# One block's output chain one scan step later, another block's keys and one value product moved, in a gated delta-rule layer on one core

## The chip, the cores and the metric

The kernel runs on one core of one Trainium2 chip. The metric is the device time of one execution in microseconds (us); the time of a kernel is the median of several executions.

## The reference

The program computes a small network on 2,048 tokens of width 128: a recurrent attention layer, a mixture of experts, a linear attention layer, and the same mixture of experts again. Every layer works on the layer norm of the residual stream and is added to it. The change touches the first layer alone:

```
def step(state, inp):
    qt, kt, vt, bt = inp
    kk = kt[..., :, None] * kt[..., None, :]
    bb = bt[..., None, None]
    state = state * (1.0 - bb * kk) + bb * (vt[..., :, None] * kt[..., None, :])
    out_t = jnp.einsum('bhij,bhj->bhi', state, qt)
    return (state, out_t)
_, outs = jax.lax.scan(step, state0, (qT, kT, vT, bT))
out = jnp.moveaxis(outs, 0, 1).reshape(b, s, nh * d)
mu = jnp.mean(out, axis=-1, keepdims=True)
var = jnp.mean((out - mu) ** 2, axis=-1, keepdims=True)
out = (out - mu) / jnp.sqrt(var + LN_EPS) * ln_g + ln_b
out = out * jax.nn.silu(x @ Wg)
return out @ Wout
```

There are 16 heads of size 8. q and k are projections divided by their norm over a head, v is a projection, beta is a sigmoid. The product of k with itself enters elementwise, so that every entry (i, j) of a head's state follows its own scalar recurrence over the tokens. The mixture of experts that follows needs, for each token, the two best of eight experts, and places its row in a table of slots with a scatter.

## The kernel before

The 2,048 tokens are cut into four blocks c of 512. A state has 16 x 8 x 8 entries: for each i of 0 to 7 the 128 pairs (head, j) lie on the partitions and the 512 tokens of a block along the rows. So there are 32 scan steps n = 8c + i, and each is written out once on every engine in a loop over n. One step n of the recurrence is:

- TensorE `repeat_v(n)`: the values, repeated for all j, into a PSUM bank (it waits for scan n - 2, which frees the bank).
- GpSimd `decay_product(n)`: the keys of index i, fetched by a DMA from a DRAM copy, times the beta keys; ScalarE `one_minus(n)` makes 1 minus that.
- VectorE `update(n)` (L1011): values times beta keys; `scan(n)` (L1020): the recurrence over 512 tokens.
- GpSimd `read_product(n)` (L502): state times q.

A block's output chain hangs on it: TensorE `sum_heads` adds the reads up, ScalarE `copy_oT` copies, TensorE `turn_o` (L1505) turns; VectorE `stats_o` (L1033), ScalarE `ln_root` (L711, into `std`), VectorE `ln_scale` (L1082 and L1084, into `rstd` and `shift`), ScalarE `normalise_o` (L699, into `otok`), TensorE `turn_n` (L1516), ScalarE `affine_nT` (L706), VectorE `open_gates` (L1040, into `gated`), TensorE `out_a`, VectorE `add_a` (L1045) and the statistics of the next layer norm, `ln_rows`, `turn_rows` (L1531), `turned_rows`, `logits`, VectorE `choose` (L1092 to L1112), TensorE `rank`, VectorE `locate` (L1118 to L1126), and at last the GpSimd scatters (L519).

The next blocks' keys are made beside it: `project_k`, `project_q`, ScalarE squares, TensorE `sum_squares` into bank 7, ScalarE `norms`, VectorE `clamp` (L970, L972), ScalarE `widen` (into `rwide`), TensorE `expand` (L1471: the norms repeated over a head), VectorE `unit_k` (L991) and `beta_k` (L998). Behind `unit_k` the DMA queue of SyncE copies the keys to DRAM and fetches the eight decays of the block.

The order on every engine is that of its loop, written out by hand. `due(n, after, first)` gives the block b with n = 8b + after, so that `due(n, 10)` puts the block's statistics in steps 10, 18, 26, 34. Within TensorE's loop body the order is `out_a`, `repeat_v`, `sum_squares`, the logits, `sum_heads`, `expand`, `turn_o`, `rank`, `turn_n`, `project_k`, `project_q`, the gate's product of steps 7 to 10, `turn_rows`. `repeat_v(n + 1)` stands in step n, but for `repeat_v(10)`, which stands in step 8. Waits that tie the chains together: `sum_squares(3)` waits for `ln_scale` of block 0's second norm (bank 7), `turn_n(1)` for `locate` of block 0 (bank 5), and on GpSimd the second four scatters of block 1 for `locate` of block 2. `PUTS` gives each scatter of a block its step: 24 to 29 for block 0; those of the other blocks stand behind the scan.

Of the kernel before, what the change touches and what calls it, by code (L numbers as in the profile page):

```python
# [27 lines left out]
HD = D // H  # L28
# [6 lines left out]
NSTEP = NB * HD  # L35
# [37 lines left out]
def program(nc, x, Wq, Wk, Wv, Wbeta, Wg, Wout, ln_g, ln_b, W_qkv, proj, W_out, b_out, w_g, c_fc, c_proj, out):  # L73
# [8 lines left out]
    with ctx:  # L82
# [83 lines left out]
        with ExitStack() as mb:  # L166
# [21 lines left out]
            b = mb.enter_context(ExitStack())  # L188
# [92 lines left out]
        last_state = lambda n: ps[:, (0, 2)[n - NSTEP + N_LAST], :]  # L281

        def due(n, after, first=0):
            b, late = divmod(n - after, HD)
            return b if late == 0 and first <= b < NB else None

# [666 lines left out]
        def _(dve):  # L953
# [13 lines left out]
            def clamp(c):  # L967
                dve.wait_ge(norm_ready, part_done(c, 1))
                dve.wait_ge(wide_ready, 2 * c)
                dve.tensor_scalar(flat(rnorm[:]), norms_in, 1e-12, None, ALU.max).then_inc(rn_clamped, 1)  # L970
                dve.wait_ge(rn_clamped, part_done(c, 1))
                dve.reciprocal(rnorm[:], rnorm[:]).then_inc(rn_ready, 1)  # L972
# [10 lines left out]
            def first_decay(i):  # L983
                dve.wait_ge(krep_ready, i + 1)
                dve.tensor_tensor(decay[:, i, :], ps[:, 6, :], bkT[:, 0, :], ALU.mult).then_inc(first_made, 1)
# [22 lines left out]
            def update(n):  # L1008
                c = n // HD
                dve.wait_ge(vrep_ready, n + 1)  # L1010
                dve.tensor_tensor(ps[:, 3 + n % 2, :], ps[:, 3 + n % 2, :], bkT[:, c % 2, :],  # L1011
                                  ALU.mult).then_inc(update_ready, 1)

            def scan(n):
                i = n % HD
                dve.wait_ge(decay_ready, n + 1)
                dve.wait_ge(update_ready, n + 1)
                if n >= HD:
                    dve.wait_ge(read_ready, n - HD + 1)
                dve.tensor_tensor_scan(out=state[:, i, :] if n < NSTEP - N_LAST else last_state(n), data0=decay[:, i, :], data1=ps[:, 3 + n % 2, :],  # L1020
                                       initial=state[:, i, BK - 1:BK], op0=ALU.mult,
                                       op1=ALU.add).then_inc(scan_done, 1)

            def read_last(n):
                dve.wait_ge(scan_done, n + 1)
                dve.wait_ge(out_ready, 2 * (NB - 2) + 2)
                dve.tensor_tensor(read[:, n % HD, :], last_state(n), qT[:, (NB - 1) % 2, :],
                                  ALU.mult).then_inc(last_read, 1)
# [48 lines left out]
            def ln_scale(n, c, moments=None):  # L1077
                tt = slice(TB * c, TB * c + TB)
                mean = mv[:, tt, 0] if moments is None else moments[:, :, 0]
                done = blocks_past(n) + (c + 1 if n < 4 else c - NB + 3)  # L1080
                dve.wait_ge(ln_std[n], done)
                dve.reciprocal(rstd[:, tt], std[:, tt]).then_inc(ln_rstd[n], 1)  # L1082
                dve.wait_ge(ln_rstd[n], done)
                dve.scalar_tensor_tensor(out=shift[:, tt], in0=mean, scalar=-1.0, in1=rstd[:, tt],  # L1084
                                         op0=ALU.mult, op1=ALU.mult).then_inc(ln_shift[n], 1)
# [63 lines left out]
            for n in range(NSTEP + 10 + HD):  # L1149
                if n < NSTEP:  # L1150
                    update(n)
                    if n == 17:
                        clamp(3)
                    scan(n)
                if n == 11:
                    ln_scale(1, 0, moments_o)
                if n == NSTEP - 1:
                    for late in range(NSTEP - N_LAST, NSTEP):
                        read_last(late)
                if n == 0:  # L1160
                    first_decay(1)
                    clamp_half(0, 0)
                if n == 1:
                    clamp_half(1, 1)
                    unit_q(0)
                if n == 2:
                    unit_k(1)
                if n == 3:
                    clamp_half(1, 0)
                if n == 4:  # L1170
                    beta_k(1)
                if n == 5:
                    unit_q(1)
                b = due(n, 17)
                if b is not None:
                    choose(0, b, logits_in(5), marks_in(5))
                b = due(n, 10)
                if b is not None:
                    stats_o(b)
                b = due(n, -6, 2)  # L1180
                if b is not None:
                    unit_k(b)
                    beta_k(b)
                b = due(n, 10)
                if b is not None and 0 < b < NB - 1:
                    ln_scale(1, b, moments_o)
                b = due(n, 18)
                if b is not None:
                    locate(0, b, ps[:, 5 if b < NB - 1 else 4, P:2 * P].rearrange("p (r t e) -> p r t e", r=4, e=NE),
                           ps[:, 5, 3 * P:3 * P + 4 * TB].rearrange("p (r t) -> p r t", r=4))  # L1190
                b = due(n, 10)
                if b == NB - 1:
                    ln_scale(1, b, moments_o)
                    normalise_late()
                b = due(n, 12)
                if b is not None:
                    open_gates(b)
                b = due(n, -3, 2)
                if b is not None:
                    unit_q(b)  # L1200
                b = due(n, 13)
                if b is not None:
                    add_a(b)
                    ln_stats(2, b, moments_a)
                b = due(n, 14)
                if b is not None:
                    ln_scale(2, b, moments_a)
                    if b == NB - 1:
                        rows_late_part(2)
                if n == 8:  # L1210
                    clamp(2)
# [201 lines left out]
        def _(pe):  # L1413
# [226 lines left out]
            for n in range(NSTEP + 10 + HD):  # L1640
                b = due(n, 13)
                if b is not None:
                    out_a(b)
                    if b == NB - 1:
                        keep_warm(30, 1)
                if 1 < n + 1 < NSTEP and n != 9:
                    repeat_v(n + 1)
                if n == 8:
                    repeat_v(n + 2)
                b = due(n, -9, 2)  # L1650
                if b is not None:
# [20 lines left out]
                b = due(n, 16)  # L1672
# [4 lines left out]
                b = due(n, 8)  # L1677
                if b is not None:
                    sum_heads(b, 1)
                b = due(n, -7, 2)  # L1680
                if b is not None:
                    expand(b)
                b = due(n, 9)
                if b is not None:
                    turn_o(b)
                b = due(n, 17)
# [4 lines left out]
                b = due(n, 11)  # L1691
# [6 lines left out]
                b = due(n, HD + -3)  # L1698
# [6 lines left out]
                b = due(n, -10, 2)  # L1705
# [18 lines left out]
                b = due(n, 15)  # L1724
# [102 lines left out]
            for gp in range(2):  # L1827
                for a_ in range(2):
                    n = 2 * gp + a_
# [103 lines left out]
```

## Time and profile before

| | |
|---|---|
| median of 3 runs | 478.07 us (477.09 to 481.09) |
| the profiled execution | 480.44 us, of which the span from its first to its last instruction is 478.6 us |
| TensorE busy | 416.2 us (87%) |
| VectorE busy | 311.5 us (65%) |
| GpSimd busy | 264.6 us (55%) |
| ScalarE busy | 235.0 us (49%) |
| mean granted clock of TensorE | 0.951 of full speed |

The rows of a trace give the start from the beginning of the span, the duration, the engine and the line of the instruction (a helper's line where a helper issues it), the tile that it writes and those that it reads, and the shapes. In square brackets stands the idle time of that engine just before, and what ended it. Engines are PE (TensorE), PEld (its weight loads), DVE (VectorE), ACT (ScalarE), POOL (GpSimd). Matmuls are pipelined: the next one starts some tenths before the recorded end of the last, and an f32 product appears as two instructions (x2).

### The profile page before, as it was taken

The page shows a single profiled execution, that of the slowest core. Times are in us where ns is not written, and L with a number is a line of the kernel's source. Part 1 is how long each engine was busy: PE and PEld are TensorE (multiplying, and loading weights), DVE is VectorE, ACT ScalarE, POOL GpSimd, SP SyncE. Part 2 cuts the span into 40 slices and gives each one's busy share as a digit, 9 for nine tenths or more (in the row PEclk, how much of TensorE's full clock was granted, in tenths as well). Part 3 has the DMA queues.
Part 4 walks back from the last instruction along what each step waited for, and adds up shares of the span by engine and source line. Part 5 has one row for each costly group of instructions (what it writes and reads, how often), then busy time and mean ns, then how long its engine had stood idle before and what let it go on. Part 6 is the DMA issues. An engine that isn't in the chain of part 4 may idle for free.

```text
span 478.6 us, 8009 instructions
## 1 busy us (share of the span) xinstructions
PE 416.2 (87%) x2850; PEld 302.3 (63%) x2850; DVE 311.5 (65%) x740; ACT 235.0 (49%) x367; POOL 264.6 (55%) x329
## 2 busy tenths in 40 slices
PE   7888796877898999999988999889878979999970
PEld 5544353333698899999964333345356969999960
DVE  5898799999753232525595999899985602421274
ACT  4777755413330355344058998878763105334320
POOL 4999675897677956465409200020656723456470
PEclk9999897775999999999999999999998999999995
DMA  5447571992161222225524444496011121232376
GB/s 144 151 163 262 165 253 53 316 322 77 41 227 50 73 85 62 68 74 207 160 83 104 100 99 100 121 285 211 24 34 46 56 80 43 59 88 61 94 241 202
DMA packets 50327, 60.88 MB, mean 127 GB/s; under 512 B 7152, under 2 KB 29296, under 8 KB 50288
## 3 DMA queue, kind: packets, MB, share of 16 engines
q1 hardware_dynamic: 42672, 47.50, 33.3%
q0 software_dynamic: 4608, 8.47, 5.5%
q10 hardware_dynamic: 3008, 4.40, 2.8%
q8 instruction: 23, 0.38, 0.3%
q14 instruction: 16, 0.13, 0.1%
HBM read 29.78 MB, written 25.31 MB: 115 GB/s over the span
## 4 chain that ended last, share of the span: by engine, by line
PE 44%; POOL 10%; issue 6%; DVE 6%; DMA 5%; ACT 4%; POOLq 0%; DVEq 0%; ACTq 0%
PE ps L1415 39%; POOL slots_x L519 8%; DVE feat L1337 3%; PE ps L1571 2%; DMA last_got<-chosen_y 1%; PE ps L1419 1%; DMA chosen_y<-ye,y_to 1%; DMA xe<-slots_x 1%; ACT expo L878 1%; POOL chosen_y L569 1%; DMA slots_x<-rows_x,put_at 1%; ACT xnT L621 1%; DVE stats L1071 1%; ACT rows_x L723 1%; POOLq L82 0%
## 5 line engine op out<-in xcount | busy, mean ns | idle before, releaser
L569 POOL DMA_INDIRECT chosen_y<-ye,y_to x80 | 79.3, 991 | 67.5 <-DVE ye L1287 48.0
L1337 DVE SCALAR_TENSOR_TENSOR feat<-expo,ps 128x1024 f32<-128x1024 f32 x64 | 76.4, 1217 | 5.6 <-ACT expo L878 5.2
L762 ACT ACTIVATE hT<-ps 128x640 f32<-128x640 f32 x64 | 45.1, 705 | 69.6 <-PE ps L1415 69.6
L519 POOL DMA_INDIRECT slots_x<-rows_x,put_at x64 | 62.9, 983 | 27.1 <-issue 16.9
L878 ACT ACTIVATE expo<-ps,minus_one 128x1024 f32<-128x1024 f32 x64 | 70.4, 1115 | 11.6 <-PE ps L1415 7.9
L1415 PE MATMUL ps<-cproj_sb,hT 128*128 128x128 f32 x640 | 74.6, 276 | 0.2
L1415 PEld LDWEIGHTS ps<-cproj_sb,hT 128*128 128x128 f32 x640 | 73.0, 192 | 0.6 <-ACT hT L762 0.6
L1419 PE MATMUL ps<-ident 128*128 128x128 f32 x546 | 66.1, 280 | 7.2 <-DMA slots_x<-rows_x,put_at 3.4
L1237 DVE TENSOR_TENSOR xe_low<-ps,xeT 128x640 fp32r<-128x640 f32 x16 | 13.2, 825 | 86.0 <-ACT xeT L621 86.0
L1419 PEld LDWEIGHTS ps<-ident 128*128 128x128 f32 x546 | 62.1, 145 | 9.7 <-DMA slots_x<-rows_x,put_at 4.3
L502 POOL TENSOR_TENSOR read<-state,qT 128x512 f32<-128x512 f32 x30 | 37.9, 1268 | 16.4 <-DVE state L1020 16.3
L1415 PE MATMUL ps<-xnT,wv_rep 128*128 128x512 f32 x64 | 40.1, 718 | 4.5 <-DVE state L1020 4.5
L1020 DVE TENSOR_TENSOR_SCAN state<-decay,state,ps 128x512 f32<-128x512 f32 x30 | 38.3, 1277 | 3.2 <-DVE ps L1011 0.5
L493 POOL TENSOR_TENSOR decay<-decay,bkT 128x512 f32<-128x512 f32 x30 | 37.8, 1267 | 0.4 <-DMA decay<-k_rows 0.4
L584 POOL TENSOR_SCALAR var_eps<-mv 128x4 f32<-128x4 f32 x2 | 0.5, 232 | 63.8 <-DVE mv L1074 63.8
L1415 PE MATMUL ps<-xeT,cfc_high 128*128 128x320 f32 x128 | 32.5, 335 | 1.9 <-ACT xeT L621 1.9
L1287 DVE TENSOR_TENSOR ye<-ps,slot_w 128x256 f32<-128x256 f32 (+2 forms) x38 | 16.6, 439 | 26.3 <-PE ps L1415 25.5
L621 ACT ACTIVATE xeT<-ps 128x640 fp32r<-128x640 f32 x16 | 11.2, 699 | 38.5 <-PE ps L1571 38.5
L1415 PE MATMUL ps<-xe_low,cfc_high 128*128 128x320 f32 x128 | 29.4, 310 | 0.0
L1415 PE MATMUL ps<-xeT,cfc_low 128*128 128x320 f32 x128 | 29.2, 309 | 0.0
L1415 PE MATMUL ps<-stk,pstk 97*128 97x512 f32 x64 | 22.6, 441 | 4.4 <-DVE feat L1337 4.3
L1415 PE MATMUL ps<-pstk,stk 97*128 97x512 f32 x64 | 23.4, 449 | 1.2 <-DVE part L1317 0.9
(238 smaller groups left out, 702.3 us busy)
## 6 DMA issues: line engine op xcount, KB each, us to landing
chosen_y<-empty_rows SPq DMA_DIRECT2D x32, 256.0 KB
decay<-k_rows SPq DMA_DIRECT2D x30, 256.0 KB, 4.8
stk<-part SPq DMA_DIRECT2D x96, 64.0 KB, 2.0
slots_x<-empty_rows SPq DMA_DIRECT2D x16, 325.0 KB, 5.9
xe<-slots_x SPq DMA_DIRECT2D x16, 325.0 KB, 2.9
cfc_sb<-in_L_ffn_c_fc SPq DMA_DIRECT2D x2, 2048.0 KB, 9.6
got<-chosen_y SPq DMA_DIRECT2D x8, 256.0 KB, 4.9
got<-chosen_y ACTq DMA_DIRECT2D x8, 256.0 KB, 5.9
```

The lines of the kernel that those rows point to most:

```text
L493: pool.tensor_tensor(decay[:, i, :], decay[:, i, :], bkT[:, c % 2, :], ALU.mult).then_inc(product_ready, 1)
L502: pool.tensor_tensor(read[:, i, :], state[:, i, :], qT[:, c % 2, :], ALU.mult).then_inc(read_ready, 1)
L519: pool.indirect_dma_start(out=slots_x[k], out_offset=bass.IndirectOffsetOnAxis(ap=put_at[:, c, kk, t:t + 1], axis=0), in_=rows_x[:, kk * N ...
L569: pool.indirect_dma_start(out=chosen_y[k], out_offset=bass.IndirectOffsetOnAxis(ap=y_to[:, b, i:i + 1], axis=0), in_=ye[:, b, i * D:(i + 1 ...
L621: copy = lambda o, i: act.activation(o, i, ACT.Copy)
L762: act.activation(hT[:, b, f, :].rearrange("p (a n) -> p a n", a=2), ps[:, 2 + 2 * (f % 2):4 + 2 * (f % 2), 0:HALF], ACT.Gelu).then_inc(h_r ...
L878: act.activation(expo[:, g % 3, :], flat(ps[:, pair, :]), ACT.Exp, bias=minus_one[:]).then_inc(f_exp, 1)
L1020: dve.tensor_tensor_scan(out=state[:, i, :] if n < NSTEP - N_LAST else last_state(n), data0=decay[:, i, :], data1=ps[:, 3 + n % 2, :], ini ...
L1287: dve.tensor_tensor(ye[:, b, i0 * D:i1 * D].rearrange("p (i d) -> p i d", d=D), ps[:, bank_of(s, n), 0:(i1 - i0) * D].rearrange("p (i d) - ...
L1337: dve.scalar_tensor_tensor(out=feat[:, g % 4, :], in0=expo[:, g % 3, :], scalar=1.0, in1=flat(ps[:, pair, :]), op0=ALU.min, op1=ALU.max).t ...
L1415: return pe.matmul(o, lhsT, rhs, start=start, stop=stop, **kw)
L1419: pe.transpose(ps[:, bank, 0:P], ident[:], ident[:])
```

## The change

Three things move, and no instruction is added or dropped.

- `due` gives, for `after` of 10 and more, block 0 one step later: everything of block 0 from `stats_o` to the scatters moves by one step on all engines (`ln_scale` of its first norm from step 11 to 12, `turn_n` from 11 to 12, `open_gates` from 12 to 13, `out_a` and `add_a` from 13 to 14, the next norm's `ln_scale` from 14 to 15, `choose` from 17 to 18, `locate` from 18 to 19, the scatters from 24 to 29 into 25 to 30). The other blocks keep their steps.
- `unit_k` and `beta_k` of block 2 move from step 10 to step 11.
- `repeat_v(11)` moves on TensorE from step 10 to step 9, ahead of `expand(2)`, `turn_o(0)` and the gate's product there.

```diff
@@ -281,6 +281,8 @@
         last_state = lambda n: ps[:, (0, 2)[n - NSTEP + N_LAST], :]
 
         def due(n, after, first=0):
+            if after >= HD + 2 and n - after < HD:
+                return 0 if n - after == 1 and first == 0 else None
             b, late = divmod(n - after, HD)
             return b if late == 0 and first <= b < NB else None
 
@@ -1152,7 +1154,7 @@
                     if n == 17:
                         clamp(3)
                     scan(n)
-                if n == 11:
+                if n == 12:
                     ln_scale(1, 0, moments_o)
                 if n == NSTEP - 1:
                     for late in range(NSTEP - N_LAST, NSTEP):
@@ -1177,7 +1179,7 @@
                 b = due(n, 10)
                 if b is not None:
                     stats_o(b)
-                b = due(n, -6, 2)
+                b = 2 if n == 11 else due(n, -6, 3)
                 if b is not None:
                     unit_k(b)
                     beta_k(b)
@@ -1643,9 +1645,9 @@
                     out_a(b)
                     if b == NB - 1:
                         keep_warm(30, 1)
-                if 1 < n + 1 < NSTEP and n != 9:
+                if 1 < n + 1 < NSTEP and n not in (9, 10):
                     repeat_v(n + 1)
-                if n == 8:
+                if n in (8, 9):
                     repeat_v(n + 2)
                 b = due(n, -9, 2)
                 if b is not None:
```

## Rows read from the trace of the kernel before

**Rows 1.** The chain that ended last (start, us, what): the end of routing.

```profile
152.95 2.41 DMA slots_x<-rows_x,put_at
```

**Rows 2.** Timeline (start, us, engine, line) of GpSimd, steps 12, 26 and behind the scan.

```profile
53.12 1.26 POOL L502 TENSOR_TENSOR read<-state,qT 128x512 f32<-128x512 f32 x1 [3.00 <-DVE state L1020]
...
105.56 1.28 POOL L502 TENSOR_TENSOR read<-state,qT 128x512 f32<-128x512 f32 x1
...
128.62 0.96 POOL L519 DMA_INDIRECT slots_x<-rows_x,put_at  x1 [2.50 <-DVE put_at L1126]
```

**Rows 3.** Timeline of VectorE, steps 9 to 12.

```profile
43.09 1.28 DVE L1020 TENSOR_TENSOR_SCAN state<-decay,state,ps 128x512 f32<-128x512 f32 x1
...
45.05 1.28 DVE L1020 TENSOR_TENSOR_SCAN state<-decay,state,ps 128x512 f32<-128x512 f32 x1
48.48 0.89 DVE L1033 BATCH_NORM_STATS2 stats<-ps 128x6 f32<-128x128 f32 x4 [2.15 <-PE ps L1505]
...
51.77 1.28 DVE L1020 TENSOR_TENSOR_SCAN state<-decay,state,ps 128x512 f32<-128x512 f32 x1
...
53.80 0.61 DVE L1084 SCALAR_TENSOR_TENSOR shift<-mean_var,rstd 128x4 f32<-128x4 f32 x1
...
57.68 0.69 DVE L1040 TENSOR_TENSOR gated<-ps,gate 128x512 f32<-128x512 f32 x1 [1.30 <-ACT ps L706]
```

**Rows 4.** What VectorE waited for, 46 to 131 us: total, times, longest.

```profile
DVE stats L1033 <- PE ps L1505: 2.1, 1, 2.1
DVE gated L1040 <- ACT ps L706: 1.3, 1, 1.3
DVE rstd L1082 <- ACT std L711: 0.9, 2, 0.5
```

**Rows 5.** Timeline of VectorE, steps 17 and 26.

```profile
69.31 0.70 DVE L1011 TENSOR_TENSOR ps<-ps,bkT 128x512 f32<-128x512 f32 x1 [0.44 <-PE ps L1415]
...
104.88 3.20 DVE L1084 SCALAR_TENSOR_TENSOR shift<-mean_var,rstd 128x4 f32<-128x4 f32 x1
```

**Rows 6.** Timeline of TensorE, steps 8 to 16.

```profile
44.53 1.02 PE L1415 MATMUL ps<-xnT,wgate 128*128 128x512 f32 x2
...
51.14 1.02 PE L1415 MATMUL ps<-xnT,wv_rep 128*128 128x512 f32 x2
55.16 1.29 PE L1516 MATMUL ps<-ident,otok 128*128 128x128 f32 x4 [3.00 <-ACT otok L699]
56.29 1.89 PE L1415 MATMUL ps<-xnT,wv_rep 128*128 128x512 f32 x2
57.96 1.90 PE L1415 MATMUL ps<-xnT,wall 128*128 128x512 f32 x2
...
65.75 1.85 PE L1415 MATMUL ps<-head_of,squares 128*128 128x16 f32 x16
...
68.25 1.02 PE L1415 MATMUL ps<-xnT,wv_rep 128*128 128x512 f32 x2
```

**Rows 7.** Timeline of ScalarE, steps 9 to 12.

```profile
47.60 0.63 ACT L681 ACTIVATE decay<-decay 128x512 f32<-128x512 f32 x1
...
54.44 1.63 ACT L699 ACTIVATE otok<-ps,shift,rstd 128x128 f32<-128x128 f32 x4 [0.89 <-DVE shift L1084]
...
56.89 0.76 ACT L706 ACTIVATE ps<-ps,lnb,lng 128x512 f32<-128x512 f32 x1
```

**Rows 8.** The instructions of L1084: duration min/median/max in ns, first and last start, forms.

```profile
L1084 DVE SCALAR_TENSOR_TENSOR shift<-mean_var,rstd x4: 161/384/3198, 53.8 to 128.5; 128x4 f32<-128x4 f32 x4
```

**Rows 9.** Busy time by stretch; third number from the right: the granted clock.

```profile
55.00:59.50 4.50, 4.30 (x8) 1.91 (x9) 3.02 (x5) 3.19 (x8) 3.10 (x3) 0.65 0.92 280
```

**Rows 10.** Timeline of TensorE, steps 19 and 20.

```profile
80.93 1.14 PE L1516 MATMUL ps<-ident,otok 128*128 128x128 f32 x4 [1.68 <-DVE put_at L1126]
82.92 2.08 PE L1415 MATMUL ps<-xnT,wv_rep 128*128 128x512 f32 x2 [0.84 <-DVE state L1020]
```

**Rows 11.** DMA issues of the whole span: KB each, median us to landing.

```profile
decay<-k_rows SPq DMA_DIRECT2D x30, 256.0 KB, 4.8
```

## The prediction

> **What bounds the kernel now.** I read the chain that ended last first. It runs without a break from the scan's last steps through block 3's output chain into the scatters, the last of which is issued at 152.95 [rows 1]; everything behind that (experts, linear attention, experts) hangs on those slots and simply moves with them. GpSimd's scatters are back to back from 128.62 on, after a wait of 2.50 for `locate` of block 2 on VectorE [rows 2]. So a microsecond that VectorE gains or loses in steps 10 to 31 goes through to the end, as long as GpSimd reaches that wait early.
>
> Then VectorE's waits: in the scan it is the engine with hardly a gap. A step with nothing beside update and scan takes 1.96 (scan starts at 43.09 and 45.05) [rows 3]. The only long waits are 2.1 for `turn_o(0)` in step 10, 1.3 for `affine_nT(0)` in step 12 and 0.5 for `ln_root(1, 0)` in step 11 [rows 4], in all 4.0. They are what moving block 0's chain touches. A fourth loss is no wait in that list: in step 26 a VectorE instruction on four elements per partition takes 3.20 [rows 5].
>
> **Part 1: step 10 emptied, `repeat_v(11)` earlier.** Scan 10 ends at 46.33 (45.05 + 1.28), and VectorE then idles 2.15 [rows 3]. In the new order `update(11)` comes next. Its values stand right behind the gate's product (44.53 to 45.55), so they are there at about 46.4, and the update ends at 47.1 [rows 6]. But scan 11 also needs `one_minus(11)`, which ScalarE does at 47.60 to 48.23, behind `widen(2)` and `copy_oT(0)`; nothing in the change moves these [rows 7]. So scan 11 starts at 48.27, with some 1.1 of new waiting. Then the statistics and keys that left step 10: from 48.48 to scan 11's update they took 2.50 (scan 11 starts at 51.77, its update 0.79 earlier at 50.98) [rows 3]; new, 49.47 + 2.50 = 51.97. `update(12)` finds `repeat_v(12)` done at 52.16, since it still stands behind the last gate product [rows 6]: 0.2 more. New waits 1.3 to 1.4 against 2.15: **gain 0.8**. Bounds: 0 (if `one_minus(11)` slips by as much again) and 2.15.
>
> **Part 2: `ln_scale(1, 0)` in step 12.** The wait of 0.54 for `std` goes: with scan 12 at 53.0 to 54.3, ScalarE has had time to load its table. Yet I count no gain. In the trace the small L1084 takes 0.61 from 53.80 and ends at 54.41, with GpSimd's read product (53.12 to 54.38) [rows 2, 3]; it reads two tiles of SBUF and was held until that read was over. The read is started by the scan's end, in the new order too, and ends 1.33 behind it. So scan end to `shift` stays 1.36. Bounds: 0 and a gain of 1.0 (0.54, and the 0.45 by which 0.61 is above the shortest, 0.16 [rows 8]), if GpSimd is late.
>
> **Part 3: `open_gates(0)` in step 13.** From `shift` (54.41) over `otok` (54.44), `turn_n` (55.16), affine (56.89) to the gate (57.68) it is 3.27 [rows 3, 6, 7]; VectorE has one bare step of 1.96 to fill it, before and after, since `ln_scale` moved by the same step as the gate. The wait of 1.30 stays: **0**. Bounds: 0 and 1.3.
>
> **Part 4: what stands behind `turn_n(0)` on TensorE.** Before, only `repeat_v(13)` stood between `turn_n(0)` and the next use by VectorE; it was over (58.18) when the gate was (58.37). New, `turn_n(0)` is in step 12 behind `repeat_v(13)`, and `project_k(3)` and `repeat_v(14)` come after it. In the new order `shift` is out at 55.63, so `turn_n` runs from 56.4 to 57.6, and the two products take 1.9 each at the lower clock, with a pitch of 1.7 (56.29 to 57.96) [rows 6], to 61.1. VectorE is done with the gate at 59.6 and with `unit_q(2)`, of about that size, at 60.1. **Loss 1.0.** The stretch 55.0 to 59.5 had a granted clock of 0.65 of full speed, mostly the 1.2 GHz level, after 3.00 without a matmul [rows 6, 9]; the new gap is 3.4, so I take the lower level. At 2.4 GHz the products take 1.02 each and the loss is 0. Bounds 0 and 1.0.
>
> **Part 5: `sum_squares(3)`, `repeat_v(17)`, `choose(0)`.** `sum_squares(3)` waits for block 0's second `ln_scale`, now in step 15 after scan 15. It takes 1.85, and `repeat_v(17)` 1.02 behind it [rows 6]. I get `update(17)` 0.85 late where it was 0.44 [rows 5]: loss 0.4. `choose(0)` in step 18 finds logits that hang on `turned_rows`, on ScalarE now behind `widen(3)`, which waits for `clamp(3)` of step 17: loss 0.25. **Loss 0.65**, bounds 0 and 1.3 (each twice).
>
> **Part 6: `turn_n(1)` behind `locate(0)`.** It was released by `locate(0)` in step 18 at 80.93, and `repeat_v(21)` had still to wait 0.84 for scan 19 [rows 10]. With `locate(0)` in step 19, both products (1.14 and, at the lower clock, 2.08, pitch 0.9 and 2.0) lie between `locate` and `update(21)`; VectorE has 1.96 for a bare step and 0.6 for the gate. **Loss 0.5**, bounds 0 and 0.5.
>
> **Part 7: scatters one step later.** The 3.20 of L1084 in step 26 starts at 104.88, while GpSimd runs scatter, read (105.56), decay product without a gap; it ends at 108.08, with the decay product [rows 2, 5]. Block 0's first three scatters are in front of it now, two after the change. GpSimd is released by scan 22 in both orders, so its offset to VectorE in step 26 is fixed: it is one scatter (1.26) ahead, and at 104.88 is 0.6 into the read, to be over at 105.6. As in part 2, L1084 then ends with that read, after 0.75: **gain 2.45**. If it is also passed over by the decay product behind, it ends at 106.8: gain 1.2. Bounds: a loss of 0.7 (a wait longer than any in the trace by that) and 3.04 (no wait). The Trainium skill (SBUF — State Buffer, Who interferes with whom) says that an instruction with two SBUF inputs contends with a GpSimd instruction that reads SBUF, and that the loser is blocked for the whole of that one instruction. The 0.61 agrees with it, the 3.20, which spans two product instructions and half a scatter, doesn't; by the rule this part gains 2.45, by the longer row 1.2 or less.
>
> The scatters are still all issued. One more now lies between scan 27 and GpSimd's wait, 1.3 and its issue gap 0.3, against a wait of 2.50 [rows 2]: 0.9 is left, so this costs nothing. If that cover were gone, each scatter too late would cost 1.3. The block's `k_rows` copy and decay DMAs on SyncE's queue start 1.0 later with `unit_k(2)`, but with the copy's 2 and a decay's 4.8 [rows 11] the first lands by 59, and scan 16 starts near 68: 0.
>
> **Sum.** 0.8 - 1.0 - 0.65 - 0.5 + 2.45 = 1.1 us less. The profiled span of 478.6 (480.44 with what lies around it) becomes 477.5; on the median of 478.07 it is **477.0**. That is no change that a measurement of this kernel can tell, which begins at about 1%, 4.8 us.
>
> **Rivals.**
> - *The held instruction is passed over again, slower:* in step 26 L1084 isn't served at the end of the read product, as in the row of 3.20, and waits 3 us once more. Then part 7 is 0 and the sum is a loss of 1.35: 479.4. It decides from a duration of 2.1 upwards in step 26 (1.1 of gain used up). For it: the same instruction at the same place did so. Against it: GpSimd is elsewhere in its sequence, and in step 11 it was served at once. Chance 0.27.
> - *TensorE keeps 2.4 GHz in steps 12 to 20:* parts 4 and 6 cost nothing: 475.5. For it: the lower clock lasted only until 59.5, and a clock that rises 1 us earlier suffices for part 4. Against it: the gap ahead of `turn_n(0)` grows. Chance 0.15.
> - *The waits go, as the change says:* parts 1 to 3 give 2.15 + 1.0 + 1.3, the losses of parts 4 to 6 hide, part 7 gives 2.45: 6.9 less, 471.2. Against it: `one_minus(11)` and the chain `shift` to gate don't move. Chance 0.10.
> - *Nothing moves but the place of the waits:* part 7 small (1.2), part 1 eaten by 4 to 6: 478.2. Chance 0.10.
>
> **How the numbers follow.** The forecast has 0.38, and its own range from the half-known parts 4 and 7 is 475.5 to 478.5. The range of 8 in 10 reaches to the slower rival and its spread and to the warm clock with part 1 whole: 473.8 to 480.0; the third rival is left out below it. Faster by over 1% is the third rival and a little of the second: 0.11. Slower by over 1% needs the slower rival and GpSimd late for `locate` too: 0.05. Within 1%: 0.84.
>
> **What would show it.** In the changed kernel's VectorE timeline: scan 11 some 1 us behind `update(11)`, released by ScalarE's decay; L1084 of block 0 ending with a read product; 1.3 ahead of L1040; an update in step 14 waiting for TensorE with the granted clock below 1; L1084 of step 26 at 0.7. I am wrong if block 0's L1084 takes 0.16, if the gate's wait shrinks, if the update of step 14 doesn't wait, or if L1084 in step 26 is again above 2.

## The result: 489.4 us, 1.9% slower, and the profile after

The changed kernel takes 489.37 us (median of 4 runs, 486.14 to 490.18) where the kernel before took 478.42 beside it (4 runs): a ratio of 1.0186 on record, with an interval of 1.0144 to 1.0227 (the quotient of these two medians alone would be 1.023). The prediction was 477.0, with a range that ended at 480.0. Lines of the changed file are those of before plus 2 (L1020 is L1022, L1084 is L1086, L1415 is L1417).

The start of a scan on VectorE's timeline cuts the span into stretches. These are the profiled executions of both kernels:

| stretch, us | before | after | difference |
|---|---|---|---|
| up to scan 10 | 45.05 | 46.83 | +1.78 |
| scan 10 to 16 | 22.54 | 23.72 | +1.18 |
| scan 16 to 22 | 22.83 | 27.09 | +4.26 |
| scan 22 to 31 | 30.14 | 30.31 | +0.17 |
| scan 31 to the end | 358.04 | 360.45 | +2.41 |
| span | 478.6 | 488.4 | +9.8 |

VectorE's timeline of the changed kernel (start, us, engine, line; in brackets the idle time before and its releaser), in the order of the prediction's parts:

```profile
50.05 1.28 DVE L1022 TENSOR_TENSOR_SCAN state<-decay,state,ps 128x512 f32<-128x512 f32 x1 [1.12 <-ACT decay L683]
...
54.06 0.70 DVE L1013 TENSOR_TENSOR ps<-ps,bkT 128x512 f32<-128x512 f32 x1 [0.38 <-PE ps L1417]
...
56.23 1.25 DVE L1086 SCALAR_TENSOR_TENSOR shift<-mean_var,rstd 128x4 f32<-128x4 f32 x1
...
60.77 0.69 DVE L1042 TENSOR_TENSOR gated<-ps,gate 128x512 f32<-128x512 f32 x1 [1.30 <-ACT ps L708]
...
63.14 0.70 DVE L1013 TENSOR_TENSOR ps<-ps,bkT 128x512 f32<-128x512 f32 x1 [1.08 <-PE ps L1417]
...
65.76 0.69 DVE L1047 TENSOR_TENSOR xres<-ps,xres 128x512 f32<-128x512 f32 x1 [0.55 <-PE ps L1417]
...
74.59 0.70 DVE L1013 TENSOR_TENSOR ps<-ps,bkT 128x512 f32<-128x512 f32 x1 [2.76 <-PE ps L1417]
...
78.60 0.70 DVE L1013 TENSOR_TENSOR ps<-ps,bkT 128x512 f32<-128x512 f32 x1 [1.04 <-PE ps L1417]
...
87.36 1.28 DVE L1022 TENSOR_TENSOR_SCAN state<-decay,state,ps 128x512 f32<-128x512 f32 x1 [0.45 <-issue]
...
92.53 0.70 DVE L1013 TENSOR_TENSOR ps<-ps,bkT 128x512 f32<-128x512 f32 x1 [0.23 <-PE ps L1417]
...
106.96 3.52 DVE L1109 TENSOR_TENSOR_SCAN upto<-later_tile,chosen 128x64 bf16<-128x64 f32 x1
...
114.23 0.95 DVE L1086 SCALAR_TENSOR_TENSOR shift<-mean_var,rstd 128x4 f32<-128x4 f32 x1
```

The last scatter of routing follows scan 31 by the same 32.4 in both orders (120.56 to 152.95 before, 127.95 to 160.35 after), so what is lost up to scan 31 goes through to it, and the 2.41 at the end come in the experts and the linear attention behind it.

The two rows with the large numbers were not in the sum as they came out: `update(17)` at 74.59 waits 2.76, where it waited 0.44 before [rows 5], and L1109, a prefix sum of 64 elements in `choose(1)`, takes 3.52 in step 25. TensorE's timeline, with its gaps at `turn_n(0)` (58.24) and `sum_squares(3)` (70.00), stands behind the first:

```profile
58.24 1.45 PE L1518 MATMUL ps<-ident,otok 128*128 128x128 f32 x4 [3.43 <-ACT otok L701]
59.48 1.92 PE L1417 MATMUL ps<-xnT,wall 128*128 128x512 f32 x2
61.19 1.91 PE L1417 MATMUL ps<-xnT,wv_rep 128*128 128x512 f32 x2
...
67.28 1.02 PE L1417 MATMUL ps<-xnT,wv_rep 128*128 128x512 f32 x2
70.00 2.66 PE L1417 MATMUL ps<-head_of,squares 128*128 128x16 f32 x16 [1.70 <-DVE shift L1086]
72.50 2.05 PE L1417 MATMUL ps<-xnT,wv_rep 128*128 128x512 f32 x2
74.48 1.94 PE L1417 MATMUL ps<-read,headsum 128*32 128x512 f32 x8
```

`sum_squares(3)` took 1.85 and the values behind it 1.02 before [rows 6]; now they take 2.66 and 2.05. Busy time by stretch (the third number from the right is the granted clock), after:

```profile
66.00:70.00 4.00, 2.30 (x6) 0.78 (x5) 3.84 (x14) 2.32 (x4) 2.12 (x3) 1.00 0.87 288
70.00:74.00 4.00, 4.00 (x18) 2.98 (x18) 1.74 (x2) 1.60 (x5) 4.00 (x4) 0.62 0.53 153
74.00:78.00 4.00, 4.00 (x15) 1.45 (x14) 2.94 (x4) 2.53 (x6) 0.96 (x2) 0.52 0.00 0
```

and before, over the same work:

```profile
63.40:75.40 12.00, 10.28 (x66) 6.12 (x64) 11.14 (x26) 8.99 (x18) 9.92 (x8) 1.00 0.52 146
```

So behind the gap of 1.70 the clock falls from 2.4 GHz to nearly the 1.2 GHz level; in the kernel before no such gap stands there, and it stays up. The second large row has GpSimd beside it; its timeline in the changed kernel:

```profile
58.82 1.27 POOL L495 TENSOR_TENSOR decay<-decay,bkT 128x512 f32<-128x512 f32 x1 [1.35 <-DMA decay<-k_rows]
...
106.58 1.21 POOL L521 DMA_INDIRECT slots_x<-rows_x,put_at  x1 [0.19 <-issue]
107.82 1.28 POOL L504 TENSOR_TENSOR read<-state,qT 128x512 f32<-128x512 f32 x1
109.04 1.27 POOL L495 TENSOR_TENSOR decay<-decay,bkT 128x512 f32<-128x512 f32 x1
...
112.68 1.25 POOL L504 TENSOR_TENSOR read<-state,qT 128x512 f32<-128x512 f32 x1 [1.19 <-DVE state L1022]
113.90 1.25 POOL L495 TENSOR_TENSOR decay<-decay,bkT 128x512 f32<-128x512 f32 x1
...
136.11 0.96 POOL L521 DMA_INDIRECT slots_x<-rows_x,put_at  x1 [1.63 <-DVE put_at L1128]
```

L1109 is asked for at 106.96, 0.38 into the first scatter, and ends at 110.48, with the decay product (109.04 + 1.27 = 110.31) and not before it. That is what L1084 did in step 26 of the kernel before [rows 5]: it ended at 108.08, its decay product at 108.05. L1107 met a product there. VectorE of the kernel before, step 25:

```profile
100.05 0.77 DVE L1107 TENSOR_TENSOR_SCAN upto<-later_tile,chosen 128x64 bf16<-128x64 f32 x1
```

and its GpSimd, the product that L1107 met, the scatter that L1084 met and the product with which L1084 ended:

```profile
99.38 1.28 POOL L493 TENSOR_TENSOR decay<-decay,bkT 128x512 f32<-128x512 f32 x1
...
104.53 1.01 POOL L519 DMA_INDIRECT slots_x<-rows_x,put_at  x1 [0.17 <-issue]
...
106.78 1.27 POOL L493 TENSOR_TENSOR decay<-decay,bkT 128x512 f32<-128x512 f32 x1
```

In the changed kernel the same small instruction of step 26 (114.23) is asked for during a product (113.90) and ends with it. GpSimd had waited 1.19 for scan 26 there, which step 25 had made late.

### The profile page after: what moved, and what is told of

Read it like the earlier page. It is cut to its first block, busy times and chain, and to the rows that moved or that the text cites. A ratio compares the mean times of both kernels' runs of the same rounds, so it can differ in the third digit from the quotient of the medians.

```text
span 488.4 us, 8009 instructions
## 1 busy us (share of the span) xinstructions
PE 420.8 (86%) x2850; PEld 306.4 (63%) x2850; DVE 313.7 (64%) x740; ACT 234.9 (48%) x367; POOL 264.5 (54%) x329
## 4 chain that ended last, share of the span: by engine, by line
PE 45%; DVE 10%; ACT 6%; DMA 5%; POOL 5%; issue 3%; ACTq 0%; POOLq 0%; DVEq 0%
PE ps L1417 40%; DVE feat L1339 4%; POOL slots_x L521 4%; PE ps L1573 2%; PE ps L1421 2%; ACT expo L880 2%; DMA last_got<-chosen_y 1%; ACT rows_x L725 1%; DMA chosen_y<-ye,y_to 1%; DMA xe<-slots_x 1%; POOL chosen_y L571 1%; DMA slots_x<-rows_x,put_at 1%; ACT xnT L623 1%; DVE stats L1073 1%; DVE xres L1366 1%
## 5 line engine op out<-in xcount | busy, mean ns | idle before, releaser
L1417 PE MATMUL ps<-cproj_sb,hT 128*128 128x128 f32 x640 | 74.6, 275 | 0.3
L1421 PE MATMUL ps<-ident 128*128 128x128 f32 x546 | 68.7, 287 | 6.5 <-POOL head_of L442 2.3
L1417 PEld LDWEIGHTS ps<-cproj_sb,hT 128*128 128x128 f32 x640 | 72.9, 192 | 0.6 <-ACT hT L764 0.6
L1421 PEld LDWEIGHTS ps<-ident 128*128 128x128 f32 x546 | 64.6, 149 | 8.8 <-DMA slots_x<-rows_x,put_at 2.9
L1417 PE MATMUL ps<-xnT,wv_rep 128*128 128x512 f32 x64 | 40.3, 726 | 2.4 <-DVE state L1022 2.4
L1022 DVE TENSOR_TENSOR_SCAN state<-decay,state,ps 128x512 f32<-128x512 f32 x30 | 38.3, 1276 | 4.5 <-ACT decay L683 1.1
L1417 PE MATMUL ps<-xeT,cfc_high 128*128 128x320 f32 x128 | 32.3, 334 | 1.9 <-ACT xeT L623 1.9
L1417 PE MATMUL ps<-xe_low,cfc_high 128*128 128x320 f32 x128 | 29.4, 311 | 0.0
L1417 PE MATMUL ps<-xeT,cfc_low 128*128 128x320 f32 x128 | 29.1, 309 | 0.0
L1013 DVE TENSOR_TENSOR ps<-ps,bkT 128x512 f32<-128x512 f32 x32 | 22.0, 687 | 7.5 <-PE ps L1417 7.2
L1417 PE MATMUL ps<-stk,pstk 97*128 97x512 f32 x64 | 22.6, 440 | 4.3 <-DVE feat L1339 4.3
```

What stands on the lines that cost most here:

```text
L1417: return pe.matmul(o, lhsT, rhs, start=start, stop=stop, **kw)
L1421: pe.transpose(ps[:, bank, 0:P], ident[:], ident[:])
```

## Experiments

Stretches on VectorE in every profiled execution, with the medians and ratios to the kernel before on the same chip. The kernel before had a median of 480.03 beside warm_squares, free_squares, after_no_lock and before_no_lock, of 480.67 beside before_again, after_again, old_scatters and after_best, and of 480.16 beside the other four. Where medians of different groups are compared below, up to 0.64 of the difference lies in that.

| kernel | scan 10 starts | 10 to 16 | 16 to 22 | 22 to 31 | sum 10 to 31 | rest | median | ratio |
|---|---|---|---|---|---|---|---|---|
| before | 45.05 | 22.54 | 22.83 | 30.14 | 75.51 | 358.04 | 478.42 | 1 |
| before_again | 46.06 | 23.37 | 22.89 | 27.07 | 73.33 | 358.51 | 481.85 | 1.0026 [0.9981, 1.0071] |
| after | 46.83 | 23.72 | 27.09 | 30.31 | 81.12 | 360.45 | 489.37 | 1.0186 [1.0144, 1.0227] |
| after_again | 48.67 | 23.92 | 27.09 | 30.41 | 81.42 | 359.11 | 488.46 | 1.0161 [1.0117, 1.0204] |
| warm_squares | 48.52 | 23.89 | 24.33 | 30.08 | 78.30 | 357.68 | 485.59 | 1.0130 [1.0093, 1.0167] |
| free_squares | 47.28 | 23.82 | 24.38 | 30.02 | 78.22 | 357.80 | 485.37 | 1.0112 [1.0011, 1.0213] |
| after_warm | 47.01 | 21.90 | 25.47 | 29.88 | 77.25 | 359.54 | 486.36 | 1.0126 [1.0059, 1.0193] |
| old_scatters | 48.73 | 23.92 | 27.10 | 27.09 | 78.11 | 358.96 | 483.04 | 1.0065 [1.0009, 1.0120] |
| after_no_lock | 47.27 | 21.67 | 24.49 | 29.13 | 75.29 | 359.54 | 483.87 | 1.0071 [1.0030, 1.0112] |
| before_no_lock | 48.49 | 22.19 | 22.90 | 27.10 | 72.19 | 359.02 | 480.72 | 1.0000 [0.9960, 1.0041] |
| after_best | 45.04 | 21.91 | 22.98 | 26.86 | 71.75 | 358.91 | 479.92 | 0.9978 [0.9937, 1.0019] |
| before_best | 45.43 | 22.18 | 22.66 | 27.25 | 72.09 | 358.38 | 478.74 | 0.9974 [0.9931, 1.0017] |
| before_warm | 45.13 | 22.54 | 23.78 | 30.12 | 76.44 | 358.33 | 479.34 | 0.9977 [0.9941, 1.0012] |
| after_best_warm | 46.10 | 20.86 | 23.42 | 28.22 | 72.50 | 359.30 | 479.00 | 0.9965 [0.9931, 0.9998] |

### Which of it repeats: both kernels once more

No edit.

> The changed kernel, once more, for its size with many runs and a second trace. Theory (the loss lies in steps 11 to 20 and is there in every execution): from scan 10 to scan 31 81.1 again, 5.6 more than before, with update(17) waiting over 2 and the small scan of step 25 at 3.5. Rival (the loss is a bad draw of the clock in one profiled execution): 78 or less, and a ratio under 1.01.

> The kernel before, once more, for a second trace of it. In the profiles so far all kernels share steps 0 to 8, yet scan 10 starts at 45.05 in the trace of before and at 46.8 to 48.5 in five others, where TensorE ran at the lower clock for a stretch around 24 to 34 us. Theory draw (when the clock drops in the first 40 us differs from execution to execution of the same program): scan 10 at 46.8 to 48.5 here too, the stretch from scan 10 to scan 31 again 75.5. Rival (the changed kernel is slower there for a reason of its own): scan 10 at 45.05 again.

Scan 16 to 22 is 27.09 in both executions of the changed kernel and 22.8 to 22.9 in both of the kernel before: this loss belongs to the change. Scan 10 to 16 is less clear: it differs by 0.83 between the two executions of the kernel before. Scan 22 to 31 shows what one profile had hidden. Before, it takes 30.14 in one execution and 27.07 in the other. The row of 3.20 that the prediction took for a fixed cost of the kernel before is missing in the second. VectorE's timeline of before_again, steps 25 and 26:

```profile
101.63 1.09 DVE L1107 TENSOR_TENSOR_SCAN upto<-later_tile,chosen 128x64 bf16<-128x64 f32 x1
...
106.47 0.16 DVE L1084 SCALAR_TENSOR_TENSOR shift<-mean_var,rstd 128x4 f32<-128x4 f32 x1
```

and of GpSimd there:

```profile
106.43 1.01 POOL L519 DMA_INDIRECT slots_x<-rows_x,put_at  x1 [0.17 <-issue]
```

L1084 is asked for 0.04 behind the scatter's start and gets through in 0.16; in the first execution it was asked for at 104.88, 0.35 behind a scatter that started at 104.53, and was held for 3.20. So a third of a microsecond decides over three. Of the three profiles of the old order with these instructions untouched, two hold L1084 for 3.20 (before and before_warm, below) and one doesn't. The changed kernel shows a held L1109 (3.52) and 30.3 to 30.4 in both of its executions.

### The gap ahead of `sum_squares(3)`: fill it, or take it away

warm_squares puts 14 transposes of the identity into the gap; free_squares gives the statistics of the second norm another PSUM bank, so that `sum_squares(3)` no longer waits for `ln_scale` of step 15:

```diff
+                if c == 3:
+                    keep_warm(14, 5)
                 pe.wait_ge(sq_ready, part_done(c, 1))
```

```diff
-        moments_a = ps[:, 7, 0:2 * TB].rearrange("p (t m) -> p t m", m=2)
+        moments_a = ps[:, 2, 0:2 * TB].rearrange("p (t m) -> p t m", m=2)
...
-                    pe.wait_ge(ln_shift[2], c - 2)
+                    pe.wait_ge(xres_a, c - 2)
```

> The changed kernel with 14 dummy transposes on TensorE in front of sum_squares(3) of step 15, in the gap of 1.70 us that its profile shows there. Theory clock (the gap drops the granted clock, and the products behind it run at the lower level): the clock stays at 1.0 from 66 to 78 us, sum_squares takes 1.85 instead of 2.66, repeat_v(17) 1.02 instead of 2.05, update(17) waits about 1 instead of 2.76, update(18) 0 instead of 1.04; some 2.5 to 3 us faster than the changed kernel. Theory order (what counts is that sum_squares(3) must wait for ln_scale of block 0 and stands in front of repeat_v(17)): update(17) waits 2 or more, and the time is that of the changed kernel.

> The changed kernel with the second norm's moments in bank 2 instead of bank 7, so that sum_squares(3) waits for add_a(0) only, not for ln_scale. Theory order: sum_squares(3) starts 1.1 us earlier (it then waits for its squares), update(17) waits 1.6 instead of 2.76. Theory clock: the gap falls to 0.6 us and with it the drop of the clock, so that update(17) waits under 1 and update(18) not at all: 3 us faster than the changed kernel. Neither touches step 25.

TensorE's timeline of warm_squares:

```profile
71.86 1.93 PE L1417 MATMUL ps<-head_of,squares 128*128 128x16 f32 x16 [0.17 <-DVE shift L1086]
73.64 1.10 PE L1417 MATMUL ps<-xnT,wv_rep 128*128 128x512 f32 x2
```

and VectorE's:

```profile
74.78 0.70 DVE L1013 TENSOR_TENSOR ps<-ps,bkT 128x512 f32<-128x512 f32 x1 [1.09 <-PE ps L1417]
```

With the gap filled the clock stays at 1.00 of full speed over 68.6 to 77.6, `update(17)` waits 1.09 instead of 2.76, `update(18)` not at all, and scan 16 to 22 falls from 27.09 to 24.33. As `sum_squares` itself starts no earlier in its step, these 2.8 us are the clock's. The median falls by 2.9. What is left of `update(17)`'s wait, 1.09, is the late start. In free_squares the gap shrinks to 0.61:

```profile
69.46 1.96 PE L1417 MATMUL ps<-head_of,squares 128*128 128x16 f32 x16 [0.61 <-ACT squares L653]
71.27 1.69 PE L1417 MATMUL ps<-xnT,wv_rep 128*128 128x512 f32 x2
```

The clock falls here too (0.74 over 69.4 to 76.0), but the products start sooner and the result is the same, 24.38. So the clock fell behind a gap of 0.61 here. It need not: in after_best, below, the same gap of 0.61 stands there, and the values behind it take 1.10. Nor need it behind the 1.70: after_no_lock, below, has that gap and keeps the clock.

### The gap ahead of `turn_n(0)`

after_warm has the transposes of warm_squares, and 28 more ahead of `turn_n(0)`:

```diff
                         pe.wait_ge(gate_ready, NB)
+                        keep_warm(28, 5)
                     turn_n(b)
```

> The changed kernel with dummy transposes in both long gaps of TensorE, 28 ahead of turn_n(0) in step 12 and 14 ahead of sum_squares(3) in step 15; its order is that of the change. Theory clock (what the changed order loses in steps 11 to 20 is the lower clock behind these two gaps): update(14) waits under 0.3 instead of 1.08 and add_a(0) not at all; from scan 10 to scan 22 46.5 instead of 50.8, near the 45.4 to 46.3 of before. Theory order: 48 as with the second gap alone.

```profile
58.34 1.39 PE L1520 MATMUL ps<-ident,otok 128*128 128x128 f32 x4 [0.30 <-ACT otok L701]
59.56 1.02 PE L1417 MATMUL ps<-xnT,wall 128*128 128x512 f32 x2
```

The two products behind `turn_n(0)` take 1.02 each instead of 1.92 and 1.91. `update(14)` and `add_a` no longer wait, and scan 10 to 16 falls by 2.0 from 23.89 to 21.90. Scan 16 to 22 gives 1.1 of that back: 0.72 of the gap ahead of `sum_squares(3)` is left behind the 14 transposes, the granted clock is 0.58 from 71.2 to 75.3, and `update(18)`, besides `update(17)`, waits 1.10. So scan 10 to 22 takes 47.37, 0.85 less than in warm_squares, where 1.7 was expected. The median, 486.36, does not show it.

### Block 0's scatters back in their old steps

```diff
-                b = due(n, 24)
+                b = 0 if n == 24 else None
...
-                    b = due(n, 24 + late)
+                    b = 0 if n == 24 + late else None
```

> The changed kernel with block 0's scatters in their old steps 24 to 29 on GpSimd, all else as changed. Theory (what the small VectorE instructions of steps 25 and 26 are held by is set by where the scatters stand): the small scan of step 25 takes 0.8 as in before and ln_scale's product of step 26 3.2; from scan 22 to scan 31 30.1 as in before, and the time is that of the changed kernel within 1 us, since one wait replaces the other. Rival (the 3.52 comes from elsewhere in the changed order): it stays above 2 with the old scatters.

VectorE's timeline, step 25:

```profile
109.06 1.09 DVE L1109 TENSOR_TENSOR_SCAN upto<-later_tile,chosen 128x64 bf16<-128x64 f32 x1
```

and GpSimd's beside it:

```profile
108.72 1.27 POOL L495 TENSOR_TENSOR decay<-decay,bkT 128x512 f32<-128x512 f32 x1
```

L1109 now meets the decay product and not the scatter, and ends with it. Scan 22 to 31 is 27.09, 3.3 less than in after_again, with scan 10 to 22 as it was (51.02 and 51.01). The median falls by 5.4 (four runs, 480.77 to 487.58), of which the profile accounts for 3.3. So the hold of L1109 comes with the moved scatters. The expectation that 3.20 in step 26 would take its place missed: L1086 is asked for 0.04 behind a scatter's start (113.90 and 113.86) and takes 0.16, as in before_again. So against an execution of the old order that passes there the second loss is 3.3, and against one that is held, as in the two first profiles, it is 0.2.

### Which instructions are held: one SBUF input instead of two

In both orders, L1084 (L1086) and L1107 (L1109) get a copy of one operand in PSUM:

```diff
+                later = flat(later_tile[:])
+                if k == 0 and c == 1:
+                    later = ps[:, 2, 2 * P:2 * P + 64]
+                    dve.tensor_copy(later, flat(later_tile[:]))
...
-                                       data0=flat(later_tile[:]),
+                                       data0=later,
```

That is the half for the prefix sum; in `ln_scale` of blocks 0 to 2 a second reciprocal writes the operand to PSUM.

> The changed kernel with one of the two SBUF inputs of ln_scale (blocks 0 to 2) and of choose's second scan (block 1) put into PSUM, by an extra reciprocal or copy of 0.2 us. Theory port (these small VectorE instructions are held while GpSimd's products read SBUF): the scan of step 25, 3.52 in the changed kernel, takes 0.3, ln_scale's product 0.16 in every block; 3 to 4 us faster than the changed kernel. Rival (the 3.52 has another cause, such as the scatter running then): it stays above 1 us.

> The kernel before with the same replacement. Theory port: the 3.20 of step 26 becomes 0.16 and the 0.77 of step 25 0.3; 2.5 to 3 us faster than before, 475.5. Rival (other cause): the time of before.

VectorE's timeline of after_no_lock:

```profile
103.19 0.29 DVE L1117 TENSOR_TENSOR_SCAN upto<-ps,chosen 128x64 bf16<-128x64 f32 x1
103.40 2.84 DVE L1122 TENSOR_TENSOR rows_x<-eight 128x4 f32<-128x4 f32 x2
```

and GpSimd's:

```profile
102.39 1.21 POOL L521 DMA_INDIRECT slots_x<-rows_x,put_at  x1 [0.17 <-issue]
103.63 1.29 POOL L504 TENSOR_TENSOR read<-state,qT 128x512 f32<-128x512 f32 x1
104.85 1.28 POOL L495 TENSOR_TENSOR decay<-decay,bkT 128x512 f32<-128x512 f32 x1
```

The prefix sum, with one input from PSUM, passes in the middle of the scatter in 0.29. The next instruction, whose two inputs both lie in SBUF, is held instead, to the end of the decay product. So at the same point of GpSimd's sequence it is the two SBUF inputs that count, not the operation. In step 26 and in block 0's `ln_scale` the instruction takes 0.16 in both orders.

The place counts too. Behind the scan, where scatters follow each other with no product behind them, the same prefix sum with both inputs in SBUF passes inside a scatter. GpSimd and VectorE of the kernel before:

```profile
125.15 0.97 POOL L519 DMA_INDIRECT slots_x<-rows_x,put_at  x1 [0.30 <-issue]
...
125.81 0.29 DVE L1107 TENSOR_TENSOR_SCAN upto<-later_tile,chosen 128x64 bf16<-128x64 f32 x1
```

It is asked for 0.66 into that scatter; in eleven profiles it was 0.21 to 0.82 into one, and took 0.29 each time. So the scatter alone holds nothing; the long holds came only where products stood behind it.

Not all that the changed kernel gains here is the hold. Scan 10 to 16 gains 2.2: L1086 is done 1.1 earlier, the gap ahead of `turn_n(0)` shrinks from 3.44 to 2.42, and the lower clock behind it ends sooner, so that `update(14)` waits 0.60 instead of 1.08 and `add_a` not at all instead of 0.75. And scan 16 to 22 falls from 27.09 to 24.49 with the gap of 1.70 still there:

```profile
68.39 1.93 PE L1425 MATMUL ps<-head_of,squares 128*128 128x16 f32 x16 [1.70 <-DVE shift L1090]
70.17 1.10 PE L1425 MATMUL ps<-xnT,wv_rep 128*128 128x512 f32 x2
```

The granted clock is 1.00 from 68.3 to 73.7, and `update(17)` waits 1.09, as in warm_squares. That bears out that the clock, and not the order, makes the difference between 27.1 and 24.4; and it shows that the gap alone doesn't decide whether the clock falls. What else does is open. In the old order the expected 475.5 missed: the median, 480.72, is level with that of the kernel before (1.0000).

### Both losses undone at once

after_best adds a PSUM copy for the held subtraction and the edit of free_squares, and moves `project_k(3)` behind the values of step 14; before_best has the PSUM copies in the old order, with the early transposes of the next section:

```diff
+                twin = eight
+                if k == 0 and c == 1:
+                    twin = ps[:, 2, 3 * P:3 * P + TB * NE].rearrange("p (t e) -> p t e", e=NE)
+                    dve.tensor_copy(twin, eight[:])
...
-                                      eight[:, :, 1 - kk], ALU.subtract)
+                                      twin[:, :, 1 - kk], ALU.subtract)
...
-                if n == 12:
+                if n == 13:
                     project_k(3)
```

> The changed kernel with sum_squares(3) freed of the wait for ln_scale, project_k(3) of step 12 put behind repeat_v(14), and all three small VectorE instructions with two SBUF inputs (ln_scale's product, choose's second scan and its subtractions in step 25) given one input in PSUM. Theory (clock and port are the whole of the loss): update(14) and update(17) wait under 0.8, steps 25 and 26 hold nothing above 0.5, from scan 10 to scan 31 under 72.5, that is 3 less than before and 8.6 less than the changed kernel; 477 to 478. Rival (more is lost in the moved chain): 74 and more, 480 and more.

> The kernel before with these transposes and with one input of the small VectorE instructions of steps 11 to 26 in PSUM. Theory port and draw: scan 10 near 45.1, from scan 10 to scan 31 72.2 as in the profile with PSUM inputs alone; 475.5. Rival (the wait of 3.20 was rare in before): 478 as with the transposes alone.

In VectorE's timeline of after_best nothing is held in step 25:

```profile
99.80 0.29 DVE L1121 TENSOR_TENSOR_SCAN upto<-ps,chosen 128x64 bf16<-128x64 f32 x1
100.00 0.20 DVE L1126 TENSOR_TENSOR rows_x<-eight,ps 128x4 f32<-128x4 f32 x2
```

Scan 10 to 31 takes 71.75, 9.7 less than in after_again, and the median, 479.92, is back at that of the kernel before. So what these edits remove is the loss. The move of `project_k(3)` has no run of its own. The moved chain brings no gain that these profiles show: with its costs gone it stands at 71.75 and 72.50 (after_best_warm, below), and the old order, with the same copies, at 72.09 (before_best).

### The start of the scan: filling TensorE's early gaps

Steps 0 to 8 are the same code in all kernels, yet scan 10 starts between 45.0 and 48.7. The granted clock in 20 to 28 us, in after_again:

```profile
20.00:28.00 8.00, 7.08 (x31) 4.70 (x31) 6.18 (x10) 4.49 (x11) 6.67 (x6) 0.79 0.59 189
```

and in after_best:

```profile
20.00:28.00 8.00, 6.50 (x32) 3.86 (x32) 7.17 (x11) 5.35 (x12) 7.58 (x7) 1.00 0.54 163
```

The execution with 0.79 starts scan 10 at 48.67, the one with 1.00 at 45.04; before_no_lock, in the old order, has 0.79 too, and 48.49. All 14 profiles fall into three groups: a clock of 0.79 in 20 to 28 and in 28 to 36 goes with 48.5 to 48.7 (four), 0.79 in 28 to 36 alone with 46.8 to 47.3 (four, the first profile of the changed kernel among them), and 1.00 in both with 45.0 to 46.1 (six). The next two kernels fill the gaps there with transposes:

```diff
                 if n == 0:
+                    keep_warm(8, 5)
                     expand(0, (0,))
...
                 if n == 3:
+                    pe.wait_ge(xnT_ready[0], NB)
+                    keep_warm(11, 6)
```

> The kernel before with 8 and 11 dummy transposes in TensorE's gaps of 0.92 and 1.27 us in steps 0 and 3. Theory draw (the kernels' spread of several us is the clock, which drops behind these gaps in some executions): scan 10 at 45.0 to 45.4 where eight profiles gave 45.0 to 48.7, granted clock 1.0 in all of 8 to 44 us, and the runs' spread halves, median 478 to 479. Rival (the draw has another cause): scan 10 anywhere up to 48.7, the spread of before.

> The changed kernel with sum_squares(3) freed, project_k(3) behind repeat_v(14), the PSUM inputs, and the transposes of steps 0 and 3. If the clock and the port were all that the change lost: from scan 10 to scan 31 71.8 as without the transposes, scan 10 near 45.1, 475.5 and level with the kernel before under the same remedies. Rival (the moved chain has a gain of its own that they uncover): 1 us or more below that kernel.

Scan 10 starts at 45.13 and 46.10 (45.43 in before_best, which has them too). That fits, in three profiles, but the medians hardly move, and the 475.5 expected of before_best and after_best_warm missed by 3. after_best_warm is below the kernel before by 0.35%, with an interval that ends 0.02% short of no change: I don't call that a faster version.

## Why the prediction was wrong

| part | forecast | measured in the profile of after against before |
|---|---|---|
| 1 step 10 emptied | -0.8 | waits 1.12 + 0.38 for 2.15: -0.65 |
| 2 `ln_scale` of block 0 | 0 | wait of 0.54 gone, L1086 1.25 for 0.61: +0.1 |
| 3 gate of block 0 | 0 | 1.30, as before: 0 |
| 4 behind `turn_n(0)` | +1.0 | `update(14)` 1.08, and `add_a` 0.55 |
| 5 `sum_squares(3)` | +0.65 | `update(17)` 2.76 for 0.44, `update(18)` 1.04: +3.4 |
| 6 behind `locate(0)` | +0.5 | `update(21)` +0.23, and 0.45 ahead of scan 19 |
| 7 step 26 | -2.45 | L1086 0.95 for 3.20: -2.25; L1109 3.52 for 0.77 in step 25: +2.75 |

**Parts 1 to 4 held in the main.** Scan 11 is released by ScalarE's decay with a wait of 1.12 (forecast 1.04); block 0's L1086 (56.23) ends with the read product; the gate waits 1.30; `update(14)` waits 1.08 with its two products at the lower clock. What was missing is `add_a`'s 0.55 (0.75 in after_again): the lower clock went one product further, into `sum_heads`. The cover named in part 7 held too: the copies of the keys made GpSimd wait 1.35 at 58.82, three steps ahead of need, and its wait for `put_at` still has 1.63 of the 2.50 [rows 2].

**Part 5 failed, in its size.** It saw that `sum_squares(3)` would wait for `ln_scale`, and priced the lateness of two products at 1.85 and 1.02. It didn't ask what TensorE does until then. The engine is through at 68.30 and idles 1.70, and part 4 had already read from [rows 6, 9] what comes behind a gap: the lower level. With 2.66 and 2.05 instead, and `sum_heads` at 1.94, the wait is 2.76 and reaches the next update as well. warm_squares shows 2.8 us of it to be the clock, and with the clock up the part comes out near its forecast of 0.65: `update(17)` waits 1.09 for 0.44, and `choose(0)` 0.24, which the later updates hid in the changed kernel. That the clock would fall could not be read from the gap with certainty (after_no_lock); it fell in after, after_again, old_scatters and free_squares.

**Part 7 failed, in its place.** The number for the instruction itself came out (0.7; it is 0.95), but by luck: the offset to GpSimd that the part took as fixed was gone, GpSimd waited 1.19 for scan 26, and L1086 ended with the decay product and not with the read. Two things more were wrong around it. The 3.20 that was to be saved is there in one execution of the kernel before and absent in another, so that against before_again nothing is saved. And the part followed one instruction only. Each instruction with two SBUF inputs that VectorE runs in steps 24 to 30 had to be set against the new order of scatters and products. L1107 stood in the trace with 0.77, where 0.29 is its time alone, ending with a product: the sign that it contends. With the sequence shifted it meets a scatter and is held for 3.52. The Trainium skill (SBUF — State Buffer, Who interferes with whom) lets the loser wait for one instruction of GpSimd. Requests during a product agree (0.95, 1.09, 1.25); those inside a scatter with products behind it don't (2.84, 3.20, 3.52): by its rule each of them would have been over within 1.3, an estimate from the products' 1.25 to 1.30.

**The rivals.** The nearest was the held instruction that is passed over again. Its mechanism came, but in step 25, where no rival looked, and together with part 5. The chance of 0.05 for slower was too small: it asked for two mishaps at once in named places, and two did come in others. The first rival's boundary of 2.1 stands too high: 0.75 and the 1.1 of gain make 1.85. It decided nothing.

**What adds up and what doesn't.** Scan 10 to 31 costs 5.6 more in the two first profiles, and 8.1 more between after_again and before_again. The medians differ by 7.8 (again) and 11. The rest lies ahead of scan 10 and behind scan 31, where the code is the same and executions of either order differ by up to 3.7 and 2.8. Without the early transposes scan 10 starts later than 46.1 in seven of eight profiles of the changed order and in one of three of the old one; whether the changed order makes late starts likelier isn't settled by so few. Nor is the 0.45 ahead of scan 19, or why GpSimd doesn't let the held instruction in between its two products.

## What to carry to other kernels

When an edit makes TensorE wait, price the products behind the wait at the lower clock as well as at the full one, down to the next place where the consumer catches up, and see whether something can fill the gap. When a sequence on GpSimd moves by one instruction, list every VectorE instruction with two SBUF inputs in that stretch, not only the one that is slow now; a PSUM copy of one input takes it out of the question. And a slow row of a single profile is no gain to be had until a second execution shows it.

## What of the hardware was not expected

- A VectorE instruction of 4 to 64 elements per partition with two SBUF inputs, asked for 0.35 to 1.0 us into a GpSimd scatter with two products behind it, was held through both: 2.84 to 3.53 us in eight profiles. At 0.04 behind the scatter's start it took 0.16 (before_again, old_scatters), and with one input in PSUM 0.29 in the middle of the scatter. With no product behind the scatter it took 0.29 with both inputs in SBUF (eleven profiles).
- The granted clock fell behind gaps of 1.70 (0.62 and then 0.52 of full speed, after) and 0.61 (0.74, free_squares) on TensorE, and in other kernels stayed at 1.00 behind the same 1.70 (after_no_lock) and the same 0.61 (after_best). The same code ahead of scan 10 had 0.79 or 1.00 of full speed in 20 to 36 us, which goes with a start of scan 10 at 48.5 to 48.7, 46.8 to 47.3 or 45.0 to 46.1, by how long the lower clock lasted.
